# One Sin in place of Sin, Abs, Sin, with the argument finished on VectorE, and four engines in a new order

## The reference

```python
q = jnp.tanh(x @ W_charge.T + b_charge)[..., 0]
phi_c = mags * q[..., None] ** jnp.arange(ORDER + 1)
shell = x @ W_shell.T + b_shell
shell = shell / jnp.maximum(jnp.linalg.norm(shell, axis=-1, keepdims=True), 1e-12)
proj = shell @ omega.T + rff_bias
phi_s = jnp.concatenate([jnp.cos(proj), jnp.sin(proj)], axis=-1) * rff_scale
tp = (phi_c[..., :, None] * phi_s[..., None, :]).reshape(b, n, -1)
phi = tp @ W_combine.T
logits = jnp.einsum('bnd,bmd->bnm', phi, phi) * T / temp
...
attn = jax.nn.softmax(logits, axis=-1)
out = jnp.einsum('bnm,bmd->bnd', attn, V)
...
topk_vals, topk_idx = jax.lax.top_k(route_logits, TOP_K)
```

## Time and profile before

| | us |
|---|---|
| median of 3 runs | 713.3 (712.23 to 713.55) |
| profiled execution | 712.14 |
| its span, first to last instruction | 709.4 |
| PE busy in the span | 679.2 (96%) |
| DVE busy | 599.2 (84%) |
| ACT busy | 516.3 (73%) |
| POOL busy | 388.9 (55%) |

### The profile page before, as it was taken

One profiled execution on the slowest core, in us unless ns is written; L12 is line 12 of the kernel. 1 busy time (PEld: TensorE's weight loads), 2 busy tenths in 40 slices (PEclk: granted clock), 3 DMA queues, 4 the chain that ended last, 5 costly groups with the idle time before them and its releaser, 6 DMA issues.

```text
span 709.4 us, 15916 instructions
## 1 busy us (share of the span) xinstructions
PE 679.2 (96%) x4636; PEld 543.3 (77%) x4636; DVE 599.2 (84%) x1953; ACT 516.3 (73%) x1506; POOL 388.9 (55%) x831
## 2 busy tenths in 40 slices
PE   9989999999999999999999999999999999998886
PEld 6857877887877968787796878778697777876664
DVE  6668978887889898888979889897988888887865
ACT  3979898768586877968686896868688695855441
POOL 3636776373646657464665657376565736535300
PEclk9999999999999999999999999999999999999999
DMA  7243020204132330413232050323214042121004
GB/s 239 96 149 91 1 61 1 61 1 144 36 119 61 102 78 18 133 32 119 61 118 62 31 141 10 120 60 121 60 61 120 2 132 48 61 61 61 2 9 169
DMA packets 49115, 54.11 MB, mean 76 GB/s; under 512 B 6212, under 2 KB 40582, under 8 KB 49030
## 3 DMA queue, kind: packets, MB, share of 16 engines
q1 hardware_dynamic: 48260, 52.57, 26.0%
q10 hardware_dynamic: 770, 0.53, 0.2%
HBM read 20.58 MB, written 16.78 MB: 53 GB/s over the span
## 4 chain that ended last, share of the span: by engine, by line
PE 69%; ACT 11%; issue 7%; POOL 5%; DVE 4%; DMA 2%; SPq 1%; DVEq 0%; ACTq 0%; POOLq 0%
PE ps L331 16%; PE ps L305 13%; PE ps L423 7%; PE ps L452 6%; PE ps L501 5%; PE ps L397 4%; PE ps L376 4%; PE ps L486 4%; PE ps L573 3%; POOL Z L242 3%; ACT L751 3%; DMA xmT<-Z 2%; PE ps L378 2%; ACT L773 2%; DVE xmL L1021 1%
## 5 line engine op out<-in xcount | busy, mean ns | idle before, releaser
L242 POOL TENSOR_TENSOR Z<-Z,QB 128x512 f32<-128x512 f32 x60 | 76.9, 1282 | 85.9 <-ACT Z L762 83.3
L703 ACT ACTIVATE xn<-X,rs 128x255 f32<-128x255 f32 x128 | 66.3, 597 | 70.2 <-POOL rs L1366 70.2
L423 PE MATMUL ps<-Vh,Eh 128*128 128x256 f32 x320 | 96.9, 303 | 1.5 <-DVE El L986 0.9
L331 PE MATMUL ps<-W1h,xh 128*128 128x354 f32 x256 | 89.3, 349 | 0.9 <-DVE xl L938 0.6
L423 PE MATMUL ps<-Vh,El 128*128 128x256 f32 x320 | 89.5, 280 | 0.0
L423 PE MATMUL ps<-Vl,Eh 128*128 128x256 f32 x320 | 89.4, 279 | 0.0
L331 PE MATMUL ps<-W1l,xh 128*128 128x354 f32 x256 | 83.2, 325 | 0.0
L331 PE MATMUL ps<-W1h,xl 128*128 128x354 f32 x256 | 83.2, 325 | 0.0
L986 DVE TENSOR_TENSOR El<-ps,Eh 128x128 fp32r<-128x128 f32 (+3 forms) x128 | 62.0, 485 | 21.4 <-ACT Eh L783 21.2
L783 ACT ACTIVATE Eh<-ps 128x128 fp32r<-128x128 f32 (+3 forms) x128 | 56.0, 450 | 32.2 <-PE ps L305 29.4
L945 DVE TENSOR_TENSOR Vl<-ps,Vh 128x256 fp32r<-128x256 f32 x128 | 53.8, 421 | 23.2 <-ACT Vh L728 21.0
(11 more groups left out here) (221 smaller groups left out, 1977.6 us busy)
## 6 DMA issues: line engine op xcount, KB each, us to landing
X<-in_x SPq DMA_DIRECT2D x32, 512.0 KB, 4.4
xmT<-Z SPq DMA_DIRECT2D x120, 128.0 KB, 2.3
out_x<-X SPq DMA_DIRECT2D x30, 512.0 KB, 2.9
out_x<-X SPq DMA_DIRECT2D x4, 256.0 KB, 2.2
X<-in_gru_whhT SPq DMA_DIRECT2D x1, 768.0 KB
...
```

The costliest lines, as they stand in the source:

```text
L242: e.tensor_tensor(Z[:, i + 1, :], Z[:, i, :], QB[:, :], ALU.mult).then_inc(s["zm"], 1)
L331: ins = e.matmul(p[:, 0:FEATS], x[:, d, c, t * 128:t * 128 + 128], w[:, c, :], start=j == 0, stop=j == 5)
L423: ins = e.matmul(p[:, 0:D], w[:, r % 2, j * 128:j * 128 + 128], v[:, (2 * k + d) % 4, j, :], start=z == 0, stop=z == len(parts) - 1)
L703: ins = e.activation(xn[:, d, t, 0:D - 1], X[:, b % NX, t, 0:D - 1], ACT.Identity, bias=rs[:, d, 2, t:t + 1], scale=rs[:, d, 1, t:t + 1])
```

## The change

`turns` on DVE is cut to the rounding alone, and three steps follow it, each with a wait for the one before: `remainder` (rounded minus `ang`, so its sign is turned), `mirror` (minus the remainder, minus 0.25) and `quarter_turn` (the larger of remainder minus 0.25 and the mirrored one, which is the absolute value minus 0.25). `sine` on ACT is then one Sin over both halves, 128x512, with scale -SCALE. The tile `quarter` and its memset go.

```diff
             def sine(k):
                 e.wait_ge(s["trig"], k + 1)
                 e.wait_ge(s["q_t"], k + 1)
-                to = PS[:, :, :, :].rearrange("p t b r -> p b t r")
-                e.activation(to[:, :, :, R:2 * R], tg[:, :, :, R:2 * R], ACT.Sin, scale=SCALE)
-                e.activation(tg[:, :, :, 0:R], tg[:, :, :, R:2 * R], ACT.Abs).then_inc(s["fold"], 1)
-                e.wait_ge(s["fold"], k + 1)
-                e.activation(to[:, :, :, 0:R], tg[:, :, :, 0:R], ACT.Sin, bias=quarter[:, 0:1],
+                e.activation(PS[:, :, :, :].rearrange("p t b r -> p b t r"), tg[:, :, :, :], ACT.Sin,
                              scale=-SCALE).then_inc(s["sin"], 1)
...
                 e.tensor_scalar(rows(tg)[:, :, 0:R], rows(ang), MAGIC, -MAGIC, ALU.add, ALU.add).then_inc(s["p3"], 1)
+
+            @live
+            def remainder(k):
                 e.wait_ge(s["p3"], k + 1)
-                e.tensor_tensor(rows(tg)[:, :, R:2 * R], rows(ang), rows(tg)[:, :, 0:R], ALU.subtract).then_inc(s["trig"], 1)
+                e.tensor_tensor(rows(tg)[:, :, R:2 * R], rows(tg)[:, :, 0:R], rows(ang),
+                                ALU.subtract).then_inc(s["rest"], 1)
+
+            @live
+            def mirror(k):
+                e.wait_ge(s["rest"], k + 1)
+                e.tensor_scalar(rows(tg)[:, :, 0:R], rows(tg)[:, :, R:2 * R], -1.0, -0.25, ALU.mult,
+                                ALU.add).then_inc(s["fold"], 1)
+
+            @live
+            def quarter_turn(k):
+                e.wait_ge(s["fold"], k + 1)
+                e.scalar_tensor_tensor(rows(tg)[:, :, 0:R], rows(tg)[:, :, R:2 * R], -0.25, rows(tg)[:, :, 0:R],
+                                       ALU.add, ALU.max).then_inc(s["trig"], 1)
```

The lists of PE, ACT, DVE and POOL are rewritten throughout, those of SP are not. Two lines of it, from POOL's loop:

```diff
-                rnorm(p); phase(p); slot_change(m); power(p, 0); power(p, 1); power(p, 2); shift8(f, 0)
-                shift8(f, 1); power(p, 3); alpha(f, 0); alpha(f, 1)
+                slot_change(m); rnorm(p); phase(p); power(p, 0); power(p, 1); power(p, 2); shift8(f, 0)
+                power(p, 3); shift8(f, 1); alpha(f, 0); alpha(f, 1)
```

More of the change, by code:

```diff
@@ L646, in _ @@
[L646 to L670, removed]
+            proj(0, 0, 0); xn_t(0, 1, 0); proj(0, 0, 1); xn_t(0, 1, 1); proj(0, 0, 2); proj(0, 0, 3)
@@ new lines, in _ @@
+            values(1, 0); proj(2, 1, 2); e_t(1, 3); proj(2, 1, 3); xm_t(0, 0, 1); values(1, 1); values(1, 2)
+            logits(1, 2); e_t(1, 4); q_t(2); xm_t(0, 1, 0); values(1, 3); e_t(1, 5); xm_t(0, 1, 1)
+            hidden(0, 0); values(1, 4); e_t(1, 6); z_t(2); values(1, 5); xn_t(3, 1, 0); hidden(0, 1)
+            proj(3, 0, 0); values(1, 6); route(0); e_t(1, 7); xn_t(3, 1, 1); rt_t(0); proj(3, 0, 1)
+            proj(3, 0, 2); phi(2); xn_t(4, 0, 0); proj(3, 0, 3); logits(2, 0); values(1, 7); proj(3, 1, 0)
@@ new lines, in _ @@
+            e_t(2, 0); e_t(2, 1); proj(3, 1, 1); proj(3, 1, 2); xm_t(1, 0, 0); proj(3, 1, 3); xm_t(1, 0, 1)
+            values(2, 0); e_t(2, 2); e_t(2, 3); logits(2, 1); gather(0); q_t(3); values(2, 1); hidden(1, 0)
+            logits(2, 2); gi_t(0); xm_t(1, 1, 0); xm_t(1, 1, 1); values(2, 2); values(2, 3); e_t(2, 4)
+            gx_rz(0); e_t(2, 5); hidden(1, 1); xn_t(4, 0, 1); z_t(3); values(2, 4); values(2, 5)
+            xn_t(4, 1, 0); route(1); e_t(2, 6); gx_n(0); proj(4, 0, 0); rt_t(1); e_t(2, 7); values(2, 6)
@@ new lines, in _ @@
+            xn_t(4, 1, 1); phi(3); values(2, 7); proj(4, 0, 1); logits(3, 0); proj(4, 0, 2); proj(4, 0, 3)
+            e_t(3, 0); proj(4, 1, 0); xm_t(2, 0, 0); e_t(3, 1); proj(4, 1, 1); proj(4, 1, 2); proj(4, 1, 3)
+            xm_t(2, 0, 1); al_t(0); slot_v(0); values(3, 0); logits(3, 1); out_mm(0, 0); gather(1); e_t(3, 2)
+            e_t(3, 3); values(3, 1); hidden(2, 0); values(3, 2); xm_t(2, 1, 0); xm_t(2, 1, 1); logits(3, 2)
+            q_t(4); e_t(3, 4); hidden(2, 1); out_mm(0, 1); gi_t(1); route(2); z_t(4); rt_t(2); gx_rz(1)
@@ L671, in _ @@
+            values(3, 3); gx_n(1); e_t(3, 5); values(3, 4); al_t(1); e_t(3, 6); values(3, 5); e_t(3, 7)
+            slot_v(1); values(3, 6); values(3, 7); phi(4); gather(2); logits(4, 0); out_mm(1, 0); gi_t(2)
             for it in range(3, 15):
@@ L908, in _ @@
+            probs_t(3, 5); route_exp(2, 0); n_tanh(1); al_copy(1); probs_t(3, 6); probs_t(3, 7)
+            route_exp(2, 1)
             for it in range(3, 15):
@@ new lines, in _ @@
+            probs_low(1, 4); inverse(1, 2); attended(1, 1); turns(2); attended(1, 2); remainder(2); mirror(2)
+            quarter_turn(2); attended(1, 3); xm_low(0, 1, 0); probs_low(1, 5); xm_low(0, 1, 1); attended(1, 4)
+            attended(1, 5); probs_low(1, 6); lm_stats(1, 1); row_max(1, 7); ln_stats(4, 1, 1); xn_low(3, 1, 0)
+            inverse(1, 3); v_low(3, 0, 0); lm_stats(1, 2); attended(1, 6); lm_stats(1, 3); top(0, 0, 0)
+            lm_stats(1, 4); top(0, 0, 1); shift(0, 0); lm_stats(1, 5); top(0, 1, 0); v_low(3, 0, 1)
@@ new lines, in _ @@
+                lm_stats(n, 1); xm_low(f, 1, 0); xm_low(f, 1, 1); turns(p); inverse(n, 2); new_slots(m)
+                remainder(p); attended(n, 2); probs_low(n, 3); mirror(p); lm_stats(n, 2); quarter_turn(p)
+                row_max(n, 6); probs_low(n, 4); row_max(n, 7); attended(n, 3); probs_low(n, 5); top(f, 0, 0)
+                top(f, 0, 1); attended(n, 4); top(f, 1, 0); shift(f, 0); top(f, 1, 1); shift(f, 1)
+                inverse(n, 3); probs_low(n, 6); attended(n, 5); probs_low(n, 7); weight_sum(f, 0)
```

249 lines of the change are left out of this document (122 added, 127 removed).

## The result

| | before | changed kernel |
|---|---|---|
| median, 6 runs of each | 713.4 us | 707.8 us (707.12 to 708.32) |
| ratio to before, 95% interval | | 0.9924 (0.9906 to 0.9941) |
| profiled execution, its span | 712.14, 709.4 | 708.32, 706.5 |
| plain pass of the loop | 40.79 | 40.25 |
| eleven passes, `phi(4)` to `phi(15)` | 450.7 | 445.5 |

The kernel is 5.6 us faster, median against median. The forecast was 708.0. The profiled execution of before lay 1.3 us under its median and that of the changed kernel 0.5 above its own, so the two profiles differ by only 3.8.

The account below looks back on a forecast made before the run. PE was taken to bound the kernel, busy 40.24 of 40.79 us per plain pass. Profiled 712.14 - 4.7 (passes) - 0.6 (start) = 706.8; with the median 1.2 above, 708.0 us; 8-in-10 range 703.5 to 714.0.

Parts of the forecast that it names:

- Where the gain is: Loop pass: a shorter Sin on ACT ends PE's wait at z_t; 0.43 us per pass with the entry, 4.7 over eleven.
- How the 0.5 is made up: Per pass on PE: 0.36 us from the wait at z_t plus 0.07 from one product entry less; e_t(n, 6) wait stays.
- The entry into the products, 0.07: PE's new order enters the three-part products (proj, values, hidden) one time less per pass, saving 0.07 us.
- The argument in time: DVE, phase to Sin: steps sum to 3.3 us, argument ready at 252.4, half a microsecond before the Sin table's load ends.
- `slot_change` moved so that the rounding is short: POOL runs slot_change before the phase, so DVE's rounding takes 0.25 us instead of 0.81.
- DVE's load costs nothing: DVE gains near 0.2 us of work per pass, costed at nothing, with no room beyond.
- from 249.1 to there: DVE's steps from the phase's end at 249.1 to probs_low(n, 6), summed to within 0.1 us of PE's new time.
- the first rival: The wait only moves: PE gives 0.36 back at e_t(n, 6) or values(n, 6); 712 to 714 us; chance 0.12.
- The start, -0.6: Ahead of the loop: first logits and expo come earlier, arguments later; -0.6 us, bounds -1.8 and +1.0.
- the loss at the second: In the start, gain at the first expo is mostly lost as xn_t(2, 0, 0) waits for the later ln_norm(2, 0).
- The end, 0: After the loop: al_t(14) fills a gap between the hidden steps but gains nothing; 0 us, bounds -0.5 and +0.5.
- The powers' waits stay 2.7: At phi in the loop: z_copy and phi both come 0.36 us earlier, so waits for moved powers stay 2.7 us.

Follow-up runs that it names:

- e10_room: Kernel before with the new arithmetic in one place, slot_change ahead of the phase on POOL and n_tanh earlier on ACT; 707.6 us.
- e2_order: Changed kernel's order on all engines with the old arithmetic (Sin, Abs, Sin on ACT; mirror and quarter_turn empty); 713.5 us.
- e4_late: Changed kernel with quarter_turn, the argument's last step, three DVE steps later in the loop; 718.2 us.
- e1_arith: Kernel before with its order kept and only the new arithmetic, all four argument steps in turns on DVE; 714.8 us.
- e3_slot: Changed kernel with POOL's slot_change put back behind rnorm and phase, beside the rounding; 708.2 us.
- e8_late1: Changed kernel with quarter_turn one DVE step later, behind row_max(n, 6); 706.0 us, and 707.2 when repeated.
- e12_same: The changed kernel run once more, unchanged; 706.7 us.

## Why the prediction was right, point by point

- **Where the gain is: right.** The pass fell by 0.54 (0.43 forecast), eleven passes by 5.1 (4.7 forecast), both in the profiled executions. PE's wait at `z_t` went, and `e10_room` had the same pass with before's order of PE and DVE. One Sin over both halves took 0.63, the value taken from the Tanh.
- **How the 0.5 is made up: partly wrong.** Medians over the passes between the same steps of PE give: first product of `proj` to `hidden` 14.23 before, 14.13 after (-0.10); wait at `z_t` 0.36 to 0 (-0.36); `z_t` to `values(n, 4)` 0.95 to 0.80 (-0.15); wait at `e_t(n, 6)` 0.39 to 0.49 (+0.10). The sum is -0.51. The wait at `e_t(n, 6)` did stay, as forecast. The prediction let PE gain no more than the 0.36 of `z_t` and left out a second wait in the same chain: `rt_t` waited for `rt_out`, which the shorter Sin brings forward as well. That is 0.13 to 0.14 of the 0.15. In each of the three kernels where `z_t` waited (before, `e2_order`, `e4_late`), `rt_t` started 0.14 behind the end of `rt_out`.
- **The entry into the products, 0.07: the size came out, the reason did not.** `e2_order` has the new order and takes 14.24 for that part, as before; `e10_room` and `e1_arith` have the old order of PE and take 14.14. The order of PE is worth nothing there. The difference lies inside the runs of products: those of 354 columns follow each other every 0.163 us in the two kernels at 14.23 and 14.24 and every 0.160 to 0.162 in all others. What the others share is that they lack the old arithmetic, with its tile `quarter` in SBUF; a version of the changed kernel with such a tile was not tried, and the cause stays open.
- **The argument in time: right, with more room than said.** 3.1 us from the end of the phase to the argument (290.17 to 293.27) where 3.3 was the sum, and 0.74 of slack where 0.5 was. Rounding and `mirror` took 0.29 and 0.28.
- **`slot_change` moved so that the rounding is short: right as a fact, worth nothing in this order.** `e3_slot` undid it, the rounding took 0.81 again, and the time did not change. The Trainium skill (SBUF — State Buffer, section Who interferes with whom) says that DVE and GpSimd share a pair of SBUF ports under an exclusive lock. The rows agree: the rounding took 0.81 beside `slot_change` and 0.29 without, in the same kernel otherwise.
- **DVE's load costs nothing: right only in the new order.** The prediction gave the passing over of this load to the sum "from 249.1 to there", and did not say what happens if the order stays. `e1_arith` shows it: the same arithmetic is worth -0.5 a pass with 0.7 us of room on DVE, and +0.2 without. My own expectation for that run, 709.4, left DVE out and missed by 5 us. It is the first rival, and it would have held in the whole kernel if the order had not made the room.
- **The start, -0.6: not seen.** In the profiled executions `phi(4)` came 0.76 later than before (182.45, 181.69). PE itself was faster: `phi(1)` could start at 67.4, as `e8_late1` shows above, where it started at 68.46 before, and the wait of 1.84 of the earlier trace rows is gone; PE waits 1.1 for `xn` and 0.8 for an `expo` instead, which is the loss at the second that was forecast. But PE then waited for moved powers, 3.8 us up to that point against 0.8. The term lay in its bounds (-1.8 and +1.0). Against the new arithmetic in the old start the new one is worth 2.7 us.
- **The end, 0: right on PE, not behind it.** From the last start of `phi` to PE's last product it is 72.21 after and 72.25 before. From the end of that product to the end of the span it is 5.9 after and 4.4 before, 1.5 more and outside the bounds of 0.5. The last four output transfers took longer to land (the last number of each row, before and after):

```profile
out_x<-X SPq DMA_DIRECT2D x4, 256.0 KB, 2.2
```

```profile
out_x<-X SPq DMA_DIRECT2D x4, 256.0 KB, 3.7
```

  This part was 5.7 to 6.1 in seven of the ten profiles with the new end and 4.7 to 4.8 in the other three; it was 4.4 to 4.8 in all four with the old one. Whether the new order has a hand in it stays open.
- **The powers' waits stay 2.7: wrong.** They were 5.9 in this profile, 5.1 in `e12_same`, and 2.1 in `e10_room`. In the nine profiles that have the changed loop and the new arithmetic they were 2.6 to 6.7, above 5 in seven; in the four with before's order of DVE and PE they were 1.4 to 2.7. So scatter alone is a weak account of it, and the cause stays open. Part of what the start gained was handed back here, and the eleven passes fell by 5.1 where 11 x 0.54 is 5.9. `e10_room` starts 2.2 us later and ends at the same time, as its eleven passes take 443.6 against 445.5. Its loop with the new start was not tried.

The forecast time came out within 0.2 us of the median, and that is partly luck. The passes are the one large term, and that one was near (-5.1 for -4.7). Of the others, in the profiled executions, the start was +0.8 for -0.6, the end +1.5 for 0, what lies outside the span -0.9 for 0, and the median lay 0.5 under the profiled execution where 1.2 above it was added. They nearly cancel. The executions of one kernel lie 1 to 4 us apart, and the same kernel once more had a median of 706.7.
